# One batch of four of a mixed weight is built on VectorE instead of GpSimd

## The chip, the cores and the metric

The kernel is one program on 1 core of a Trainium2 chip. The metric is its device time in microseconds, the median of several runs. The engines are TensorE (PE in the profile, with its weight loads as PEld), VectorE (DVE), ScalarE (ACT), GpSimd (POOL) and SyncE (SP).

## The reference, cut to what matters

The whole computation is a transformer of four layers over x of 16 batches, 128 tokens and 128 features, with a conditioning vector of 8 numbers for each batch. Layer 0 reads, in short:

```python
x = x + _L0_attn_ref(_L0_cond_ref(x, cond_8, ...), Wq, Wk, Wv, Wo, ...)
x = x + _L0_ffn_ref(_L0_cond2_ref(x, cond_8, weight, mask, bias), w_gate, w_up, w_down)
```

The attention has 16 heads of 8 features. What the change touches belongs to the second line: `_L0_cond2_ref` multiplies the tokens of batch b by a weight that is a mixture of 8 matrices `weight[g]` (128x128) with the factors `cond_8[b, g]`, times a common `mask`. As the kernel writes it, transposed, with W8[g] = weight[g] * mask:

```python
WBOT[b] = sum(cond_8[b, g] * W8[g] for g in range(8))   # 16 batches, 128x128 each
y[b] = x[b] @ WBOT[b] + bias
```

## The kernel before

Activations lie in SBUF with the features on the partitions, 16 batches of 128 tokens in columns, worked on in NC = 4 chunks n of 4 batches (512 columns). The program is one list of steps, `order`, written while the kernel is built. Each engine walks the same list and issues its own part of each step in that order, so a step that stands earlier in the list stands earlier in every engine's queue. Waits between engines are semaphores, and buffers in rings (`Ring`, take and give) carry the signal after which they may be used again.

`in_order` makes the list as a software pipeline. An item is a list of stages. In each round one new item starts, and then every item that is under way does its next stage, the youngest first.

In the attention of layer 0 (`mh_attn(0, ...)`) an item is half of a group of heads: 4 chunks x 4 groups j x 2 halves = 32 items. The stages of one, with their lines:

- scores: TensorE, four products (L1660) into two PSUM banks of the ring RA, which has four banks. The keys are masked copies `kb`, made by GpSimd (L2721, four instructions for each two items, ring of three).
- row maximum and exponential: VectorE reduces both banks (L2251, twice) and subtracts the maximum in the first one (L2254); ScalarE takes exponentials of the second bank straight from PSUM (L1960, four), and of the first from SBUF (L1963). The banks come free after L2254 and after L1960.
- turn: TensorE transposes (L1587, L1588), ScalarE copies to SBUF (L1968).
- values and sums: TensorE (L1676, L1680).
- in every second item VectorE takes a reciprocal and multiplies (L2261, L2263), and at the end of a chunk TensorE projects (L1687) and VectorE adds the result to X (L2266).

Between the head items stand items for the next chunk: the conditioned weight (VectorE L2159, TensorE L1609, VectorE L2164, TensorE L1615), queries and keys (TensorE L1625, L1626, VectorE L2146), and values (VectorE L2217, TensorE L1631, VectorE L2244).

Beside the heads runs other work, one piece for each head item. `beside_heads` appends it to the first stage, behind the scores: first `wmask` (VectorE, L2269, which makes W8), then the 32 `wbot` steps (b = 0, 4, 8, 12, and for each b all g = 0 to 7), the last two in the 32nd item. In items 3 and on there is also a step of the feed-forward weights' quantization (`fq`, VectorE, L2275 to L2287), or of the routing (L2185 to L2210, and the multiply-add of L2146 on SM). So on VectorE whatever a head item has beside it stands before the row maximum of the item before.

A `wbot` step is GpSimd's alone. It multiplies W8[g], spread over four batches, by their four factors spread over 128 columns (L2731, a 128x512 product), for g > 0 into a scratch tile of the ring RWB, and then adds this to WBOT (L2735, also 128x512). WBOT is read by `cond2` (L1700), four products for each chunk, the first of which stand behind the last head items.

Of the kernel before, what the change touches and what calls it, by code (L numbers as in the profile page):

```python
# [115 lines left out]
def bc_mid(ap, n):  # L116
    return ap.rearrange("p (a b) -> p a b", a=1).broadcast_to([ap.shape[0], n, ap.shape[1]])
# [26 lines left out]
def build(nc, xT, cst, l0b, w8, b2, fw, fd, l1c, moe1, l1f, moe2, moe3, l2f, moe4, l3f, xs, ys, out):  # L144
    with ExitStack() as ctx:
# [29 lines left out]
        def c(name, rows=128):  # L175
            a, w = CL[name]
            return CC[0:rows, a:a + w]
# [31 lines left out]
        def tick(name, by=1):  # L209
            s = S_(name)  # L210
            counts[name] += by
            return s, counts[name]
# [5 lines left out]
        def step(kind, **at):  # L218
            order.append((kind, at))
            return at  # L220
# [353 lines left out]


        WBOT = A1[:, 8192:10240].rearrange("p (b o) -> p b o", b=16)
        RWB = Ring([A1[:, 10240 + 512 * k:10752 + 512 * k] for k in range(2)])
        WUG = BW[:, 6144:6912].rearrange("p (n o) -> p n o", o=128)
        WDN = BW[:, 6912:7296].rearrange("p (n o) -> p n o", o=128)

        def wbot_steps():
            def masked():
                sig["wmask"] = tick("wmask")
                step("wmask")
            steps = [masked]
            for b in range(0, NB, 4):
                for g in range(8):
                    def go(b=b, g=g):
                        at = step("wbot", b=b, g=g, mask=sig["wmask"], prev=sig.get(("wb", b)), tmp=RWB.take() if g else None)
                        at["part"] = sig["wb", b] = sig["wbot"] = tick("wbot_pool")  # L590
                        if g:
                            at["acc"] = sig["wb", b] = sig["wbot"] = tick("wbot_pool")
                            RWB.give(at["tmp"], at["acc"])
                    steps.append(go)
            return steps
# [35 lines left out]

        for n in range(NC):
            def c2(n=n):
                at = step("cond2", n=n, x=sig["x0", n], wbot=sig["wbot"], pa=RA.take(),
                          yfree=sig["Yfree", n])
                at["mm"] = sig["wbot_over"] = tick("c2_mm")
                at["y"] = sig["y0b", n] = tick("c2_y")
                RA.give(at["pa"], at["y"])
            items.append(([("x0", n)], [c2], ("y0b", n)))
# [937 lines left out]
        def _(e):  # L1577
# [27 lines left out]
            for kind, at in order:  # L1605
# [88 lines left out]
                elif kind == "cond2":  # L1694
                    over(at["pa"])
                    w.wait_ge(*at["wbot"])
                    w.wait_ge(*at["x"])
                    for j in range(4):
                        b = 4 * at["n"] + j
# [434 lines left out]
        def _(e):  # L2134
# [17 lines left out]
            for kind, at in order:  # L2152
# [114 lines left out]
                elif kind == "wmask":  # L2267
                    w.wait_ge(*loaded["w8"])
                    e.tensor_tensor(W8, W8, bc_mid(c("maskT"), 8), ALU.mult).then_inc(sig["wmask"][0], 1)  # L2269
                elif kind == "fq":  # L2270
                    k, mx, iv = at["k"], at["mx"], at["iv"]
                    r3 = at["raw"].rearrange("p (n k) -> p n k", k=32)
# [423 lines left out]
        def _(e):  # L2696
# [6 lines left out]
            for kind, at in order:  # L2703
# [18 lines left out]
                    i.then_inc(at["t"][0], 1)  # L2722
                elif kind == "wbot":
                    b, g = at["b"], at["g"]
                    to = WBOT[:, b:b + 4, :]
                    yb = COND.rearrange("p (b g) -> p b g", g=8)[:, b:b + 4, g]
                    part = v4(at["tmp"].ap) if g else to
                    w.wait_ge(*at["mask"])
                    if g:
                        over(at["tmp"])  # L2730
                    e.tensor_tensor(part, bc_mid(W8[:, g, :], 4), bc_last(yb, 128), ALU.mult).then_inc(at["part"][0], 1)  # L2731
                    if g:
                        w.wait_ge(*at["part"])
                        w.wait_ge(*at["prev"])
                        e.tensor_tensor(to, to, part, ALU.add).then_inc(at["acc"][0], 1)  # L2735
                elif kind == "f0_magic":
                    w.wait_ge(*loaded["cst2"])
# [144 lines left out]
```

## Time and profile before

| | us |
|---|---|
| median of 3 runs | 1372.43 |
| lowest and highest | 1371.03, 1373.96 |
| the profiled execution, its own time | 1373.96 |
| its span (first to last instruction) | 1372.10 |
| granted clock over the span | 0.978 of full |
| PE busy | 1245.3 |
| DVE busy | 839.9 |
| ACT busy | 666.9 |
| POOL busy | 283.7 |

How to read it: busy time is a sum over the whole span, of stages with different limits. Times in views of the trace count from the start of the span. An idle time in brackets at the end of a timeline row is that of the engine just before the row, with the instruction that ended it. Matmuls are pipelined, so rows of TensorE can overlap.

### The profile page before, as it was taken

What the parts mean: (1) busy time and instruction counts of PE and PEld (TensorE: products, weight loads), DVE (VectorE), ACT (ScalarE), POOL (GpSimd) and SP (SyncE); (2) the same over time, 40 slices, a digit from 0 to 9 for tenths busy, and PEclk for the clock granted to TensorE, in tenths of its full rate; (3) what the DMA queues carried; (4) which work ended last, traced back from release to release, by engine and by line L of the source; (5) the groups of instructions that cost most, each with busy time, mean ns of one, the idle gap of its engine ahead of it and who ended that gap; (6) DMA issues with size and microseconds to landing.
All of it is one profiled execution on the core that took longest, in us unless ns stands there. A gap on an engine that the chain in (4) does not pass through costs nothing.

```text
span 1372.1 us, 26279 instructions
## 1 busy us (share of the span) xinstructions
PE 1245.3 (91%) x9327; PEld 965.1 (70%) x9327; DVE 839.9 (61%) x1781; ACT 666.9 (49%) x1346; POOL 283.7 (21%) x379
## 2 busy tenths in 40 slices
PE   6999962889999899999999999899999999998999
PEld 2555621468788799887878887698889655556777
DVE  4888678564555567567776564666554666754242
ACT  2666687345434234443444444244444466655553
POOL 5877300210004143220000022233400211100000
PEclk9999986999999999999999999999999999999999
DMA  9000100501222122105034002032020000000000
GB/s 320 2 2 1 43 36 0 207 1 62 104 105 89 57 84 77 43 18 208 1 133 180 1 16 60 25 110 64 28 87 1 1 2 1 2 1 1 0 16 16
DMA packets 42892, 75.69 MB, mean 55 GB/s; under 512 B 3848, under 2 KB 33808, under 8 KB 41872
## 3 DMA queue, kind: packets, MB, share of 16 engines
q1 hardware_dynamic: 38672, 65.62, 13.2%
q0 software_dynamic: 4096, 8.40, 2.1%
q8 instruction: 80, 1.31, 0.4%
q14 instruction: 44, 0.36, 0.1%
HBM read 59.72 MB, written 14.29 MB: 54 GB/s over the span
## 4 chain that ended last, share of the span: by engine, by line
PE 75%; DVE 13%; ACT 7%; issue 3%; DMA 1%; DVEq 1%; POOL 0%; ACTq 0%; SPq 0%; POOLq 0%
PE bank L1811 8%; PE bank L1822 7%; PE bank L1807 7%; PE bank L1866 5%; PE bank L1660 4%; PE bank L1798 4%; PE bank L1587 4%; PE bank L1876 3%; PE bank L1592 3%; PE bank L1593 3%; PE bank L1594 2%; PE bank L1791 2%; PE bank L1793 2%; PE bank L1792 2%; PE bank L1676 2%
## 5 line engine op out<-in xcount | busy, mean ns | idle before, releaser
L2059 ACT ACTIVATE SC<-bank 128x512 f32<-128x512 f32 x192 | 114.4, 596 | 222.4 <-PE bank L1807 124.8
L2146 DVE SCALAR_TENSOR_TENSOR SC<-bank,SM,SC 128x512 f32<-128x512 f32 x128 | 95.8, 748 | 122.6 <-PE bank L1811 101.0
L1822 PE MATMUL bank<-A,SC 128*128 x1024 | 137.0, 277 | 7.8 <-DVE SC L2146 7.1
L1807 PEld LDWEIGHTS bank<-X,SC 128*128 128x128 f32 x1024 | 127.0, 193 | 19.3 <-issue 13.0
L1811 PE MATMUL bank<-X,SC 128*128 128x128 f32 x1024 | 137.3, 277 | 3.3 <-DVE SC L2420 2.7
L1807 PE MATMUL bank<-X,SC 128*128 128x128 f32 x1024 | 136.9, 277 | 3.2 <-ACT SC L2043 2.5
L1822 PEld LDWEIGHTS bank<-A,SC 128*128 128x128 f32 x1024 | 125.5, 192 | 17.1 <-issue 16.3
L1811 PEld LDWEIGHTS bank<-X,SC 128*128 128x128 f32 x1024 | 125.4, 193 | 5.4 <-DVE SC L2420 5.2
L1866 PE MATMUL bank<-A 128*128 128x128 f32 x736 | 100.2, 280 | 11.2 <-DVE A L2570 6.2
L1960 ACT ACTIVATE A<-bank,SM 128x128 f32<-128x128 f32 x256 | 73.8, 383 | 58.0 <-DVE SM L2251 57.8
L1866 PEld LDWEIGHTS bank<-A 128*128 128x128 f32 x736 | 90.1, 193 | 15.4 <-ACT A L2084 8.9
L2721 POOL TENSOR_SCALAR A<-A,CC 128x256 f32<-128x256 f32 (+1 forms) x128 | 55.0, 450 | 214.0 <-DVE A L2238 108.8
L2043 ACT ACTIVATE SC<-A 128x512 f32 x128 | 80.6, 630 | 28.5 <-PE bank L1811 22.8
L2771 POOL DMA_INDIRECT A<-ys,POSI x64 | 62.7, 980 | 130.0 <-PE bank L1860 38.4
L2759 POOL DMA_INDIRECT xs<-CC,POSI x64 | 64.2, 1003 | 115.8 <-DVE POSI L2549 28.1
L2251 DVE TENSOR_REDUCE SM<-bank 128x4 f32<-128x512 f32 x128 | 81.8, 680 | 7.9 <-PE bank L1660 6.4
L2400 DVE TENSOR_TENSOR SC<-bank,SC 128x512 f32<-128x512 f32 x64 | 44.3, 692 | 62.5 <-PE bank L1793 52.1
L1660 PE MATMUL bank<-A 64*128 64x512 f32 (+1 forms) x256 | 73.7, 653 | 8.3 <-POOL A L2721 3.7
L1587 PEld LDWEIGHTS bank<-CC,A 128*128 128x128 f32 x408 | 46.8, 142 | 43.9 <-issue 16.1
L1876 PE MATMUL bank<-BW,A 128*128 x552 | 77.2, 277 | 0.0
L1592 PE MATMUL bank<-R 128*128 128x512 f32 x176 | 69.4, 394 | 7.6 <-DVE SC L2146 6.1
L2746 POOL TENSOR_TENSOR SM<-SM 128x32 f32<-128x32 f32 x32 | 8.3, 259 | 314.4 <-DVE SM L2146 312.5
(322 smaller groups left out, 2586.1 us busy)
## 6 DMA issues: line engine op xcount, KB each, us to landing
A<-in_moe SPq DMA_DIRECT2D x36, 768.0 KB, 10.3
A<-xs SPq DMA_DIRECT2D x20, 256.0 KB, 4.0
ys<-A SPq DMA_DIRECT2D x20, 256.0 KB, 2.3
BW<-in_l1f SPq DMA_DIRECT2D x2, 2048.0 KB, 7.5
BW<-in_l2f SPq DMA_DIRECT2D x1, 3456.0 KB, 12.2
BW<-in_l1c SPq DMA_DIRECT2D x1, 3072.0 KB, 17.3
BW<-in_l3f SPq DMA_DIRECT2D x1, 2816.0 KB, 9.7
A<-in_l1c SPq DMA_DIRECT2D x1, 2560.0 KB, 8.7
```

Source lines behind the costliest of these rows:

```text
L1587: e.transpose(o[:, cut(r)], i[:, cut(r)], ident)
L1592: e.matmul(o, wh, hi, start=start, stop=False)
L1660: m = e.matmul(pa.ap, q[rows, a:a + 128], kb[rows, b:b + 512], start=at["i"] == 0, stop=True)
L1807: m = e.matmul(at["pg"].ap[:, cut(q)], wx[:, cut(q)], x, start=True, stop=True)
L1811: m = e.matmul(at["pu"].ap[:, cut(q)], wx[:, cut(4 + q)], x, start=True, stop=True)
L1822: m = e.matmul(o, at["h"].ap[:, cut(q)], W[:, bass.ds(r + (1024 + 128 * q), 128)], start=k == 0 and q == 0, stop=k == 1 and q == 3)
L1866: m = e.matmul(at["pa"].ap[:, cut(q)], at["wt"].ap[:, cut(q)], at["x"].ap, start=True, stop=True)
L1876: m = e.matmul(o, at["ht"].ap[:, cut(q)], BW[:, bass.ds(r + (dn + 128 * q), 128)], start=q == 0, stop=q == nk - 1)
L2043: e.activation(at["wx"].ap[0][:, 0:512], MOE_AT[at["L"]][:, bass.ds(r, 512)], ACT.Identity).then_inc(at["g"][0], 1)
L2059: e.activation(at["h"].ap, at["pg"].ap, ACT.Gelu_apprx_tanh).then_inc(at["gelu"][0], 1)
L2146: return e.scalar_tensor_tensor(out=o, in0=a, scalar=s, in1=b, op0=o1, op1=o2)
L2251: e.tensor_reduce(m[:, 4 * x:4 * x + 4], v4(pa.ap), AX, ALU.max, negate=True).then_inc(at["max"][x][0], 1)
```

## The change

In each `wbot` step, GpSimd does batches b+1 to b+3 (128x384 instead of 128x512) and VectorE does batch b itself: one 128x128 instruction, a `tensor_scalar` for g = 0 and a `scalar_tensor_tensor` (W8[g] times the factor, plus WBOT) for g > 0. Both have two semaphore counters now, `wbot_dve` for VectorE and `wbot_pool` for GpSimd, each engine waits for its own earlier sum alone, and `cond2` waits for both. The scratch tiles have 384 columns instead of 512. `stt(o, a, s, b, o1, o2)` is `e.scalar_tensor_tensor`, as VectorE's other code uses it.

```diff
--- before.py
+++ after.py
@@ -574,7 +574,7 @@
 
 
         WBOT = A1[:, 8192:10240].rearrange("p (b o) -> p b o", b=16)
-        RWB = Ring([A1[:, 10240 + 512 * k:10752 + 512 * k] for k in range(2)])
+        RWB = Ring([A1[:, 10240 + 384 * k:10624 + 384 * k] for k in range(2)])
         WUG = BW[:, 6144:6912].rearrange("p (n o) -> p n o", o=128)
         WDN = BW[:, 6912:7296].rearrange("p (n o) -> p n o", o=128)
 
@@ -586,10 +586,12 @@
             for b in range(0, NB, 4):
                 for g in range(8):
                     def go(b=b, g=g):
-                        at = step("wbot", b=b, g=g, mask=sig["wmask"], prev=sig.get(("wb", b)), tmp=RWB.take() if g else None)
-                        at["part"] = sig["wb", b] = sig["wbot"] = tick("wbot_pool")
+                        at = step("wbot", b=b, g=g, mask=sig["wmask"], prev=sig.get(("wb", b)), prev_pool=sig.get(("wb3", b)),
+                                  tmp=RWB.take() if g else None)
+                        at["t"] = sig["wb", b] = sig["wbot"] = tick("wbot_dve")
+                        at["part"] = sig["wb3", b] = sig["wbot_pool"] = tick("wbot_pool")
                         if g:
-                            at["acc"] = sig["wb", b] = sig["wbot"] = tick("wbot_pool")
+                            at["acc"] = sig["wb3", b] = sig["wbot_pool"] = tick("wbot_pool")
                             RWB.give(at["tmp"], at["acc"])
                     steps.append(go)
             return steps
@@ -631,7 +633,7 @@
 
         for n in range(NC):
             def c2(n=n):
-                at = step("cond2", n=n, x=sig["x0", n], wbot=sig["wbot"], pa=RA.take(),
+                at = step("cond2", n=n, x=sig["x0", n], wbot=sig["wbot"], wbot_pool=sig["wbot_pool"], pa=RA.take(),
                           yfree=sig["Yfree", n])
                 at["mm"] = sig["wbot_over"] = tick("c2_mm")
                 at["y"] = sig["y0b", n] = tick("c2_y")
@@ -1694,6 +1696,7 @@
                 elif kind == "cond2":
                     over(at["pa"])
                     w.wait_ge(*at["wbot"])
+                    w.wait_ge(*at["wbot_pool"])
                     w.wait_ge(*at["x"])
                     for j in range(4):
                         b = 4 * at["n"] + j
@@ -2267,6 +2270,15 @@
                 elif kind == "wmask":
                     w.wait_ge(*loaded["w8"])
                     e.tensor_tensor(W8, W8, bc_mid(c("maskT"), 8), ALU.mult).then_inc(sig["wmask"][0], 1)
+                elif kind == "wbot":
+                    b, g = at["b"], at["g"]
+                    y = COND[:, 8 * b + g:8 * b + g + 1]
+                    w.wait_ge(*at["mask"])
+                    if g == 0:
+                        e.tensor_scalar(WBOT[:, b, :], W8[:, g, :], y, None, ALU.mult).then_inc(at["t"][0], 1)
+                    else:
+                        w.wait_ge(*at["prev"])
+                        stt(WBOT[:, b, :], W8[:, g, :], y, WBOT[:, b, :], ALU.mult, ALU.add).then_inc(at["t"][0], 1)
                 elif kind == "fq":
                     k, mx, iv = at["k"], at["mx"], at["iv"]
                     r3 = at["raw"].rearrange("p (n k) -> p n k", k=32)
@@ -2722,16 +2734,16 @@
                     i.then_inc(at["t"][0], 1)
                 elif kind == "wbot":
                     b, g = at["b"], at["g"]
-                    to = WBOT[:, b:b + 4, :]
-                    yb = COND.rearrange("p (b g) -> p b g", g=8)[:, b:b + 4, g]
-                    part = v4(at["tmp"].ap) if g else to
+                    to = WBOT[:, b + 1:b + 4, :]
+                    yb = COND.rearrange("p (b g) -> p b g", g=8)[:, b + 1:b + 4, g]
+                    part = at["tmp"].ap.rearrange("p (b o) -> p b o", b=3) if g else to
                     w.wait_ge(*at["mask"])
                     if g:
                         over(at["tmp"])
-                    e.tensor_tensor(part, bc_mid(W8[:, g, :], 4), bc_last(yb, 128), ALU.mult).then_inc(at["part"][0], 1)
+                    e.tensor_tensor(part, bc_mid(W8[:, g, :], 3), bc_last(yb, 128), ALU.mult).then_inc(at["part"][0], 1)
                     if g:
                         w.wait_ge(*at["part"])
-                        w.wait_ge(*at["prev"])
+                        w.wait_ge(*at["prev_pool"])
                         e.tensor_tensor(to, to, part, ALU.add).then_inc(at["acc"][0], 1)
                 elif kind == "f0_magic":
                     w.wait_ge(*loaded["cst2"])
```

## Rows read from the trace of the kernel before

**Rows 1.** The page, part 1: busy time and share of the span of each engine.

```profile
PE 1245.3 (91%) x9327; PEld 965.1 (70%) x9327; DVE 839.9 (61%) x1781; ACT 666.9 (49%) x1346; POOL 283.7 (21%) x379
```

**Rows 2.** The chain that ended last between 26 and 147 us, shares by line.

```profile
by line: PE bank L1660 24.9%; PE bank L1587 17.5%; PE bank L1676 10.4%; PE bank L1680 8.0%; PE bank L1625 5.3%; PE bank L1588 4.9%; ACT A L1960 4.6%; PE bank L1626 4.3%; DVE SM L2251 3.0%; PE bank L1609 2.5%; PE bank L1715 2.4%; PE bank L16
```

**Rows 3.** Windows: us, busy (count) of PE, PEld, DVE, ACT, POOL, clock, DMA.

```profile
26.00:147.00 121.00, 114.58 (x1291) 68.82 (x1289) 101.00 (x222) 79.02 (x207) 96.21 (x117) 0.99 0.07 19
...
118.00:142.00 24.00, 22.87 (x308) 14.04 (x300) 21.75 (x84) 18.91 (x52) 23.37 (x29) 1.00 0.01 3
```

**Rows 4.** Groups of GpSimd by line and shape, 26 to 160 us: count, busy, mean.

```profile
L2735 POOL TENSOR_TENSOR A<-A 128x512 f32<-128x512 f32 x28 | 36.6, 1307 | 2.2
L2731 POOL TENSOR_TENSOR A<-A,CC 128x512 f32<-128x512 f32 x32 | 34.8, 1087 | 0.0
L2721 POOL TENSOR_SCALAR A<-A,CC 128x256 f32<-128x256 f32 x57 | 27.1, 495 | 22.6 <-PE bank L1588 9.0 <-DVE A L2146 8.2 <-PE bank L1660 5.3
```

**Rows 5.** Timeline of GpSimd: start, us, line, operation, idle before.

```profile
61.89 1.27 POOL L2735 TENSOR_TENSOR A<-A 128x512 f32<-128x512 f32 x1
63.13 1.76 POOL L2731 TENSOR_TENSOR A<-A,CC 128x512 f32<-128x512 f32 x1
...
133.92 1.85 POOL L2721 TENSOR_SCALAR A<-A,CC 128x256 f32<-128x256 f32 x4
...
146.28 1.28 POOL L2735 TENSOR_TENSOR A<-A 128x512 f32<-128x512 f32 x1
```

**Rows 6.** Timeline of TensorE.

```profile
54.22 1.13 PE L1660 MATMUL bank<-A 64*128 64x512 f32 x4 [1.62 <-ACT A L1960]
...
56.62 1.13 PE L1660 MATMUL bank<-A 64*128 64x512 f32 x4 [0.24 <-issue]
...
73.17 1.10 PE L1625 MATMUL bank<-Y,CC 128*128 128x512 f32 x2 [0.91 <-ACT A L1960]
...
88.94 1.13 PE L1660 MATMUL bank<-A 64*128 64x512 f32 x4 [0.18 <-ACT A L1960]
...
138.41 1.13 PE L1660 MATMUL bank<-A 64*128 64x512 f32 x4
...
146.60 1.13 PE L1660 MATMUL bank<-A 64*128 64x512 f32 x4
...
152.79 1.16 PE L1700 MATMUL bank<-X,A 128*128 128x128 f32 x8
```

**Rows 7.** Timeline of ScalarE (ACT).

```profile
55.37 1.14 ACT L1960 ACTIVATE A<-bank,SM 128x128 f32<-128x128 f32 x4 [0.78 <-DVE SM L2251]
...
87.65 1.14 ACT L1960 ACTIVATE A<-bank,SM 128x128 f32<-128x128 f32 x4
...
137.04 1.14 ACT L1960 ACTIVATE A<-bank,SM 128x128 f32<-128x128 f32 x4 [0.54 <-DVE SM L2251]
```

**Rows 8.** Timeline of VectorE (DVE).

```profile
49.94 0.29 DVE L2263 TENSOR_TENSOR A<-bank,A 128x128 f32<-128x128 f32 x1
50.15 1.54 DVE L2281 TENSOR_TENSOR A<-A,SM 128x768 f32<-128x768 f32 x1
...
61.99 1.99 DVE L2287 TENSOR_TENSOR A<-A,SM 128x768 f32<-128x768 f32 x1
...
69.96 0.69 DVE L2266 TENSOR_TENSOR X<-bank,X 128x512 f32<-128x512 f32 x1 [2.40 <-PE bank L1687]
...
96.05 1.25 DVE L2281 TENSOR_TENSOR A<-A,SM 128x384 f32<-128x384 f32 x1
...
113.37 0.55 DVE L2287 TENSOR_TENSOR A<-A,SM 128x384 f32<-128x384 f32 x1
...
118.70 0.96 DVE L2261 RECIPROCAL A<-bank 128x128 f32<-128x128 f32 x1 [0.60 <-PE bank L1680]
...
121.69 0.57 DVE L2185 CAST IDB<-CC 128x128 bf16<-128x128 f32 x1
...
135.39 0.42 DVE L2146 SCALAR_TENSOR_TENSOR SM<-SM 128x32 f32<-128x32 f32 x1
```

## The prediction

> **What bounds the kernel now.** I read the page first. TensorE is busy for 91% of the span and GpSimd (POOL) for 21% [rows 1]: over the whole kernel TensorE is the bound, and GpSimd is not. But the change touches one stage, the attention of layer 0 with its 32 head steps, from about 26 to 147 us. So the windows of that stage come next. There VectorE (DVE) is busy 101.00 of 121 us, GpSimd 96.21, TensorE 114.58, and between 118 and 142 us VectorE is busy 21.75 and GpSimd 23.37 of 24 us, with TensorE at full granted clock, 1.00 (2.4 GHz) [rows 3]. Both engines between which work is moved are nearly full. Which one matters is told by the chain that ended last: in this stretch its shares are TensorE's, then ACT's exponential L1960 at 4.6% and VectorE's row maximum L2251 at 3.0%, and no GpSimd line is among the shares shown [rows 2].
>
> Is GpSimd on the path anywhere? It makes two things that TensorE needs: the masked keys (L2721), and WBOT. The last four-instruction group of masked keys starts at 133.92, ends 1.85 us later at 135.77, and feeds a scores product that starts at 146.60, after the one at 138.41 has used the group before it. WBOT is finished at 146.28 + 1.28 = 147.56 [rows 5] and first read by L1700 at 152.79 [rows 6]. GpSimd has 5.2 us to spare at WBOT and about 11 us at the keys. What is taken from it shortens nothing directly.
>
> VectorE has no such room. TensorE idles where a scores product waits for a PSUM bank, which comes free when ACT has done the four L1960, which wait for VectorE's L2251 of the same head. At 54.22 TensorE had idled 1.62 us for L1960. At 56.62 it starts 0.11 us after the L1960 that began at 55.37 (55.37 + 1.14 = 56.51), and that one had waited 0.78 us for VectorE. At 88.94 it is the same (87.65 + 1.14 = 88.79), and so at one earlier product, near 44 us. At 138.41 the product starts 0.23 us after the end of the L1960 that began at 137.04, itself held up 0.54 us by VectorE [rows 6, 7]. The handoff takes 0.10 to 0.15 us in the cases where TensorE idles, so about 0.1 us is slack.
>
> **The change, part by part.** GpSimd's two instructions per step go from four batches to three, from 128x512 to 128x384. Before they took 34.8 us (x32, mean 1.087) and 36.6 us (x28, mean 1.307) [rows 4]. I scale by elements, an estimate: 0.79 and 0.95 us at the undisturbed 1.05 and 1.27. That frees some 17 us of GpSimd, worth nothing by itself, since its cover is the 5.2 and 11 us above. The added wait of L1700 for a second semaphore is also worth nothing: VectorE's last slice, at the 32nd head step, stands in its queue before row maxima that finish before 152.79. The two scratch buffers only shrink.
>
> VectorE gets 32 instructions of 128x128, one in each head step: 4 multiplications by a scalar and 28 multiply-adds (scalar_tensor_tensor) of WBOT. Each is queued before the row maximum of the head before, on the chain above. Its own occupancy: L2263, 128x128 on VectorE, has 0.29 us and the next instruction starts 0.21 us after it (49.94 to 50.15) [rows 8]. I take 0.21.
>
> To that comes a wait. The new instructions read two operands from SBUF, and so does L2281 (a tile of A times a strip of SM). At 96.05 a 128x384 L2281 took 1.25 us, while L2287 on the same shape with GpSimd idle took 0.55 at 113.37: 0.70 more. At 61.99 the 128x768 L2287 took 1.99 us. Its undisturbed time, from 0.55 plus 384 elements at (0.55-0.29)/256 us each, is 0.94: 1.05 more. In that moment GpSimd ran L2735 from 61.89 to 63.16, and then an L2731 that took 1.76 instead of 1.05 [rows 5, 8]. VectorE stood until GpSimd's instruction ended, ran, and held up GpSimd's next one. At 50.15 it is 1.54 - 0.94 = 0.60 more, for the 128x128 cast at 121.69 0.57 - 0.29 = 0.28. For the 128x32 multiply-add at 135.39, 0.42 against 0.19 (0.29 less 96 elements) is 0.23 more. Mean of the five: 0.57 us. That a multiply-add of two SBUF operands does it too is told by the last of these.
>
> The Trainium skill, SBUF — State Buffer, section "Who interferes with whom", says the same of the pair of ports that VectorE and GpSimd share: an instruction of VectorE with two SBUF inputs and one of GpSimd that reads SBUF exclude each other for the whole instruction. By that rule the move cannot be free while GpSimd works; by the rows alone it is 0.23 to 1.05 us for each that meets it. The Trainium skill, Perfetto Trace Analysis, section "Optimizing Scalar/DVE Operations", adds that offloading between these two might not help for this reason; the trace agrees in these five rows.
>
> How often do they meet? If the new instruction comes at a random moment, its mean wait is the sum over GpSimd's instructions of count times duration squared, over twice the 121 us: (32 x 0.79^2 + 28 x 0.95^2 + 57 x 0.46^2) / 242 = (20.0 + 25.3 + 12.1) / 242 = 0.24 us (0.46 is one of the four instructions of the 1.85 us at 133.92). Bounds: no wait, 0; always a meeting like those measured, 0.57. I take 0.24, since most of those measured were long enough to be caught and GpSimd's instructions are now shorter. One new instruction then costs w = 0.21 + 0.24 = 0.45 us, between 0.21 and 0.78. All 32 are 14.4 us of VectorE.
>
> How many lie on the path? I count them at each place where TensorE waits for VectorE, from the last idle moment of VectorE before it: before the product near 44 us, one; before 54.22, one; before 56.62, one more; at 69.96 VectorE adds to X after an idle time of 2.40 us, and the step's new instruction stands between it and the row maximum whose L1960 lets TensorE start at 73.17 after 0.91 us of idling [rows 6, 8]: one; before 88.94 one, and one more for the product after it; the same addition to X one chunk later: one. Then from 118.70 on VectorE has no idle time in its queue until that release at 138.41 is past. The new instructions of head steps 22 to 27 stand there before the row maximum that releases 138.41: six. Together 1+1+1+1+2+1+6 = 13. The other 19 fall into idle times of VectorE, or where TensorE has 0.4 to 2 us in hand. 13 x 0.45 = 5.85 us.
>
> Off goes slack: 0.1 at 138.41 and about 0.4 at the others together, 0.5 (an estimate). Off goes relief: the waits of VectorE's old instructions on this path (0.60 at 50.15, 0.28 at 121.69, 0.23 at 135.39: 1.1) shrink with GpSimd's instructions to about three quarters: 0.3. Sum: 5.85 - 0.5 - 0.3 = +5.05 us. A check from capacity: 118 to 142 us has 2.25 us of VectorE free and gets 8 x 0.45 = 3.6, so it must grow by at least 1.35 us; the path count gives 6 x 0.45 - 0.1 = 2.6. Behind the stage everything moves as a block, for I see nothing with its own due time.
>
> The profiled execution was 1373.96 us (span 1372.1), 1.5 above the median of 1372.43. The sum makes it 1379.0; against the median, 1372.43 + 5.05 = 1377.5.
>
> **The rivals.** (A) The forecast: 1377.5, own range 1375.2 to 1379.5.
>
> (B) VectorE absorbs it. For: 19 of 32 are already counted as hidden, and GpSimd gets gaps in which nobody waits for it. Then w is 0.21 at the same 13 places: 2.7 - 0.8 = +1.9, 1374.4; if places drop out as well, 1372.4. Against: GpSimd is busy 23.37 of 24 us in the densest stretch now [rows 3], and its work there falls only by a fifth or so.
>
> (C) The waits bunch. VectorE's new instruction is caught each time, as the long ones were (w = 0.78): 13 x 0.78 = 10.1, less 0.5 is +9.6, 1382.0. For: five rows of such waits. Against: the means of rows 4 (1.087 and 1.307 against 1.05 and 1.27) show that most of GpSimd's instructions met nobody, and the new ones are short.
>
> (D) Faster: the relief outweighs the load. Mechanism: GpSimd catches up with its queue and idles while VectorE runs its long two-operand instructions, so all 1.1 us of old waits on the path go, and L2281 at 96.05 and L2287 at 61.99 lose another 1.75 between them: up to -2.85, 1369.6. It decides only if w at the 13 places is nearly nothing, under 2.85/13 = 0.22, that is without any wait and with some of the places hidden. For it: both engines share what they contend for. Against: the occupancy of 0.21 alone eats it. The other way to be faster, that GpSimd was late, is excluded by 5.2 and 11 us of room.
>
> (E) The Trainium skill, GPSIMD Engine Reference, section "Engine selection", prefers VectorE for elementwise work, GpSimd being about twice as slow with two inputs. That is an advantage in engine time: some 17 us of GpSimd freed against 32 x 0.21 = 6.7 us of VectorE. As a time it would show only through (D), and is counted there.
>
> **How the numbers follow.** No change can be told from a change under 0.2%, 2.7 us here. Chances: A 0.45, B 0.32, C 0.15, D 0.08. A and C end slower; of B 0.05 too, when w lies between; of D 0.05 is faster and 0.03 within. Slower 0.65, same 0.30, faster 0.05. The likeliest is A: 1377.5. The range leaves out the upper part of C and most of D, and B below 1373: 1373.0 to 1381.5.
>
> **What would show it.** Right: 32 new DVE rows of 128x128, many longer than 0.3 us, their ends on ends of GpSimd's instructions; GpSimd's two groups at about 0.8 and 0.95 us; the first L1700 about 5 us later than 152.79, and the time behind it unchanged; VectorE's idle time between 118 and 145 us gone, and TensorE's waits for L1960 longer there. Wrong: the new rows all near 0.2 us (B); TensorE's waits for L1960 not longer, so that the count of 13 was too high; the first L1700 earlier (D); or a second place that moves, behind 170 us, which the block shift excludes.

## The result, and the profile after

The changed kernel took 1379.76 us (median of the first 6 runs, 1378.61 to 1387.59), the kernel before 1372.16 in the same series. The ratio of its runs to those of the kernel before on the same chip is 1.007, 95% interval 1.0052 to 1.0089: 9.6 us slower, between 7.1 and 12.2. It was run again beside the experiments: over all 25 runs, the first six among them, its median is 1381.83 and its range 1376.71 to 1387.59. So the direction was forecast and the size was not: +5.05 us against 7.6 (medians) to 9.6 (ratio). The median of the first six lies in the range of 1373.0 to 1381.5, the ratio times 1372.43, 1382.0, lies outside.

The spread itself is new: 11 us over 25 runs, where the 73 runs of the kernel before beside them have 6 (1368.71 to 1374.57). It goes with TensorE's granted clock. The runs with a granted clock of 0.980 over the span took 1376.7 to 1379.7 us, those with 0.975 or 0.974 took 1384.5 to 1387.6. The kernel before lies at 0.978 or above in 72 of the 73. A part of this lies far behind the stage of the change: the profiled execution of the kernel before was granted 0.91 of full clock from 260 to 280 us and 0.93 from 455 to 480 and from 615 to 640, that of the changed kernel 1.00 in all three. So one execution compared with one other can be off by some us, and where it matters below the stage is compared by itself.

The page after, part 1, as in [rows 1]:

```profile
PE 1245.9 (90%) x9327; PEld 963.3 (70%) x9327; DVE 852.2 (62%) x1813; ACT 667.2 (48%) x1346; POOL 268.1 (19%) x379
```

The windows after, as in [rows 3], and one more stretch:

```profile
118.00:142.00 24.00, 21.93 (x286) 13.98 (x284) 23.58 (x88) 16.42 (x44) 23.26 (x34) 1.00 0.01 2
142.00:160.00 18.00, 14.19 (x156) 8.76 (x154) 12.88 (x26) 9.92 (x27) 3.09 (x4) 0.81 0.01 2
```

The same stretch of the kernel before:

```profile
142.00:160.00 18.00, 17.12 (x233) 12.10 (x234) 11.42 (x19) 13.41 (x35) 5.40 (x5) 1.00 0.01 2
```

From 118 to 142 us VectorE has gone from 21.75 to 23.58 us busy. From 142 to 160 TensorE was granted 0.81 of full clock, where it had 1.00. GpSimd's groups by shape, 24 to 170 us, as in [rows 4]:

```profile
L2747 POOL TENSOR_TENSOR A<-A 128x384 f32<-128x384 f32 x28 | 29.2, 1042 | 2.2
L2743 POOL TENSOR_TENSOR A<-A,CC 128x384 f32<-128x384 f32 x32 | 26.8, 839 | 0.0
```

VectorE's new instructions, the 28 multiply-adds and the 4 multiplications:

```profile
L2149 DVE SCALAR_TENSOR_TENSOR A<-A,CC 128x128 f32<-128x128 f32 x28 | 14.7, 526 | 0.0
...
L2278 DVE TENSOR_SCALAR A<-A,CC 128x128 f32<-128x128 f32 x4 | 1.7, 428 | 0.0
```

GpSimd's two groups are at 0.839 and 1.042 us (0.79 and 0.95 forecast). The new instructions have means of 0.526 and 0.428 us.

TensorE's timeline, as in [rows 6]. The product of 54.22 is now at 54.83, 56.62 at 58.11, 88.94 at 91.36, 118.56 at 121.00, 138.41 at 145.01, and the first product of WBOT of 152.79 (L1703 now) at 162.24:

```profile
54.83 1.45 PE L1662 MATMUL bank<-A 64*128 64x512 f32 x4 [2.05 <-ACT A L1963]
...
58.11 1.51 PE L1662 MATMUL bank<-A 64*128 64x512 f32 x4
...
77.81 1.13 PE L1662 MATMUL bank<-A 64*128 64x512 f32 x4
...
91.36 1.13 PE L1662 MATMUL bank<-A 64*128 64x512 f32 x4 [0.73 <-ACT A L1963]
...
121.00 1.13 PE L1662 MATMUL bank<-A 64*128 64x512 f32 x4
...
145.01 2.08 PE L1662 MATMUL bank<-A 64*128 64x512 f32 x4 [2.94 <-DVE A L2257]
...
151.39 1.12 PE L1689 MATMUL bank<-A,CC 128*128 128x512 f32 x2
...
162.24 1.16 PE L1703 MATMUL bank<-X,A 128*128 128x128 f32 x8
```

At 145.01 TensorE had idled 2.94 us, and its scores step (the row of four) then took 2.08 us instead of 1.13. The granted clock was 0.56 of full from 144 to 146 us and 0.50, which is the lower level of 1.2 GHz, from 146 to 150. From there to the projection L1689 at 151.39 it needs 6.38 us. Before, the same work took from 138.41 to 141.94, 3.53 us:

```profile
118.56 1.13 PE L1660 MATMUL bank<-A 64*128 64x512 f32 x4
...
141.94 1.13 PE L1687 MATMUL bank<-A,CC 128*128 128x512 f32 x2
```

So the delay grows in three parts: 2.44 us up to 118.56, 4.16 more up to 138.41 (6.60 in all), and 2.85 more at the lower clock (9.45 in all at the first product of WBOT).

What VectorE did in the idle time, and GpSimd beside it:

```profile
136.75 1.28 DVE L2254 TENSOR_REDUCE SM<-bank 128x4 f32<-128x512 f32 x2
...
138.55 1.17 DVE L2149 SCALAR_TENSOR_TENSOR A<-A,CC 128x128 f32<-128x128 f32 x1
138.56 1.00 POOL L2747 TENSOR_TENSOR A<-A 128x384 f32<-128x384 f32 x1
...
139.52 0.89 POOL L2743 TENSOR_TENSOR A<-A,CC 128x384 f32<-128x384 f32 x1
...
139.64 0.80 DVE L2207 TENSOR_SCALAR SM<-SM 128x16 f32<-128x16 f32 x1
...
140.47 0.25 DVE L2209 RECIPROCAL SM<-SM 128x16 f32<-128x16 f32 x1
140.48 1.00 POOL L2747 TENSOR_TENSOR A<-A 128x384 f32<-128x384 f32 x1
...
140.76 0.76 DVE L2211 TENSOR_TENSOR SM<-SM 128x16 f32<-128x16 f32 x1
...
141.44 0.83 POOL L2743 TENSOR_TENSOR A<-A,CC 128x384 f32<-128x384 f32 x1
141.55 0.76 DVE L2213 TENSOR_SCALAR SM<-SM 128x32 f32<-128x32 f32 x1
142.34 0.19 DVE L2149 SCALAR_TENSOR_TENSOR SM<-SM 128x32 f32<-128x32 f32 x1
142.35 1.04 POOL L2747 TENSOR_TENSOR A<-A 128x384 f32<-128x384 f32 x1
142.45 1.28 DVE L2254 TENSOR_REDUCE SM<-bank 128x4 f32<-128x512 f32 x2
...
143.77 1.14 ACT L1963 ACTIVATE A<-bank,SM 128x128 f32<-128x128 f32 x4 [3.07 <-DVE SM L2254]
```

The row maxima (L2254) start at 136.75 and next at 142.45. Between them stand the new instruction (1.17 us) and five tiny instructions that make the routing weights from 16 or 32 columns. Each depends on the one before. The new instruction ends when GpSimd's L2747 (138.56 to 139.56) has ended, L2207 ends at 140.44, just before GpSimd's next begins, L2211 at 141.52 and L2213 at 142.31, each time at the end of an instruction of GpSimd or in the gap before the next. So three of the five wait for what is left of an instruction of GpSimd. The reciprocal L2209 and the last one, L2149, do not. In the kernel before, this chain happened to run beside the masked keys, 0.46 us each [rows 5, the row at 133.92], and ended with the row at 135.39 [rows 8]:

```profile
134.35 0.16 DVE L2204 TENSOR_SCALAR SM<-SM 128x16 f32<-128x16 f32 x1
134.55 0.25 DVE L2206 RECIPROCAL SM<-SM 128x16 f32<-128x16 f32 x1
134.84 0.20 DVE L2208 TENSOR_TENSOR SM<-SM 128x16 f32<-128x16 f32 x1
135.07 0.28 DVE L2210 TENSOR_SCALAR SM<-SM 128x32 f32<-128x32 f32 x1
```

1.46 us from 134.35 to 135.81 there, 2.89 us from 139.64 to 142.53 here: 1.43 us more.

### The profile page after: what moved, and what is told of

Its sections match the earlier page's. It is cut to its first block, busy times and chain, and to the rows that moved or that the text cites. A ratio compares the mean times of both kernels' runs of the same rounds, so it can differ in the third digit from the quotient of the medians.

```text
span 1378.9 us, 26311 instructions
## 1 busy us (share of the span) xinstructions
PE 1245.9 (90%) x9327; PEld 963.3 (70%) x9327; DVE 852.2 (62%) x1813; ACT 667.2 (48%) x1346; POOL 268.1 (19%) x379
## 4 chain that ended last, share of the span: by engine, by line
PE 71%; DVE 16%; ACT 7%; issue 4%; DVEq 1%; DMA 1%; POOL 0%; ACTq 0%; SPq 0%; POOLq 0%
PE bank L1814 7%; PE bank L1825 7%; PE bank L1810 7%; PE bank L1869 5%; PE bank L1801 4%; PE bank L1662 4%; PE bank L1589 3%; PE bank L1879 3%; PE bank L1594 3%; PE bank L1596 2%; PE bank L1595 2%; PE bank L1794 2%; DVE SM L2254 2%; PE bank L1796 2%; PE bank L1795 2%
## 5 line engine op out<-in xcount | busy, mean ns | idle before, releaser
L2149 DVE SCALAR_TENSOR_TENSOR SC<-bank,SM,SC 128x512 f32<-128x512 f32 x128 | 95.9, 749 | 122.1 <-PE bank L1814 95.6
L2254 DVE TENSOR_REDUCE SM<-bank 128x4 f32<-128x512 f32 x128 | 81.9, 681 | 8.5 <-PE bank L1662 7.2
L1879 PEld LDWEIGHTS bank<-BW,A 128*128 128x128 f32 x552 | 69.3, 192 | 2.0 <-issue 1.9
## 6 DMA issues: line engine op xcount, KB each, us to landing
BW<-in_l2f SPq DMA_DIRECT2D x1, 3456.0 KB, 12.2
```

Source lines behind the costliest of these rows:

```text
L1879: m = e.matmul(o, at["ht"].ap[:, cut(q)], BW[:, bass.ds(r + (dn + 128 * q), 128)], start=q == 0, stop=q == nk - 1)
L2149: return e.scalar_tensor_tensor(out=o, in0=a, scalar=s, in1=b, op0=o1, op1=o2)
L2254: e.tensor_reduce(m[:, 4 * x:4 * x + 4], v4(pa.ap), AX, ALU.max, negate=True).then_inc(at["max"][x][0], 1)
```

## The experiments

All ratios are against runs of the kernel before on the same chip, in the same series. "Head stage" below is the time from the third scores step (33.23 us before) to the first product of WBOT (152.79), in the profiled execution: 119.6 us before, 129.1 after the change. It leaves out what differs in start and rest from one execution to the next, but it is read from one execution of each kernel.

**r1: GpSimd's share left out.** Batches b+1 to b+3 are zeros, VectorE's instructions stay.

```diff
+ e.memset(WBOT[batches b+1 to b+3], 0.0).then_inc(t_wzero[0], 1)     # once, at the start
- GpSimd: both instructions of every wbot step
```

> The changed kernel, but GpSimd's share of WBOT (batches b+1 to b+3) is left out: zeros are written there once at the start, so that share of the computation is missing. VectorE's 32 instructions stay. Port theory (the loss comes from waits of VectorE for GpSimd's running instruction, which end in idle TensorE and then in half clock): the 28 multiply-adds fall from a mean of 0.53 us to 0.34 (the value of those that met nobody), the old waits go as well, no TensorE idling over 2 us in the head stage, time 1370 to 1374 us. Occupancy theory (the 32 instructions' own time on the path is what costs): about 11 places x 0.26 = +2.9 at least stays and, with the clock drops unchanged, the time is 1376 to 1380 us.

Measured: 1375.2 us (12 runs), ratio 1.0021 (1.0011 to 1.0031): +2.9 us. Head stage 120.6 us. VectorE's group of new instructions:

```profile
L2148 DVE SCALAR_TENSOR_TENSOR A<-A,CC 128x128 f32<-128x128 f32 x28 | 10.4, 372 | 0.0
```

The same 28 instructions take 0.372 us each, not 0.526. With GpSimd's share gone nearly nothing is left to wait for, so +2.9 us (1.5 to 4.2) is about what their occupancy costs. In the profiled execution only 1.1 us of it lies in the head stage; where the rest lies was not found. The port theory's time was 1.2 us too low, since it took no occupancy into account, and the occupancy theory's 1376 to 1380 was 0.8 too high.

**r2: the new instructions cannot wait.** VectorE reads one operand only.

```diff
- stt(WBOT[:, b, :], W8[:, g, :], y, WBOT[:, b, :], ALU.mult, ALU.add)
+ e.tensor_reduce(RED[:, k:k + 1], W8[:, g, :], AX, ALU.max)
```

> The changed kernel with each of VectorE's 32 new instructions replaced by a maximum over one 128x128 slice of W8, written to a column of its own: one SBUF operand, about the same length. Batch b of each four is left out of WBOT (zeros written once at the start). GpSimd's share is as in the changed kernel. Port theory: the new instructions show about 0.25 us each with no spread, VectorE's old two-operand instructions still wait, time 1373 to 1376 us. Occupancy theory: as the changed kernel, 1379 to 1382 us.

Measured: 1378.99 us (5 runs), ratio 1.0051 (1.0038 to 1.0064): +7.0 us. The port theory as I had put it falls here, and the time is at the lower end of the occupancy theory's. The new instructions take 0.274 us and meet nobody, and yet most of the loss is there. The trace suggested another cause. VectorE's routing chain:

```profile
137.47 0.73 DVE L2210 TENSOR_SCALAR SM<-SM 128x16 f32<-128x16 f32 x1
138.24 0.25 DVE L2212 RECIPROCAL SM<-SM 128x16 f32<-128x16 f32 x1
138.53 0.76 DVE L2214 TENSOR_TENSOR SM<-SM 128x16 f32<-128x16 f32 x1
139.31 0.76 DVE L2216 TENSOR_SCALAR SM<-SM 128x32 f32<-128x32 f32 x1
140.11 0.19 DVE L2152 SCALAR_TENSOR_TENSOR SM<-SM 128x32 f32<-128x32 f32 x1
```

and TensorE afterwards:

```profile
142.78 1.13 PE L1665 MATMUL bank<-A 64*128 64x512 f32 x4 [1.71 <-DVE A L2260]
```

The chain has moved from 134.35 to 137.47 and takes 2.83 us instead of 1.46: here it is old instructions that wait, because the new ones push them onto GpSimd's instructions of 0.83 to 1.0 us. This gave the theory that r10 and r14 test. It does not explain all of this run: the head stage is 122.7 us, 3.1 more than before, and the other 4 us of the +7.0 lie outside it. TensorE also kept full clock after its 1.71 us of idling.

**r3: GpSimd's share alone.** VectorE's 32 instructions are gone, batch b is zero.

> The changed kernel without VectorE's 32 instructions: batch b of each four is left out of WBOT (zeros written once at the start), GpSimd does three batches of 384 columns as in the changed kernel. Both theories: GpSimd's shorter instructions alone cost nothing, 1370.5 to 1372.5 us, a little faster than before as the old waits shrink (0.3 us). Rival (the shift in phase between the two engines is itself the cause of the convoy of small routing instructions near 140 us): 1375 us or more.

Measured: 1371.8 us (11 runs), ratio 0.9997 (0.9988 to 1.0006). Head stage 119.5 us. Shortening GpSimd's instructions is worth nothing clear of the noise, as forecast (between 1.6 us faster and 0.8 slower).

**r4: VectorE's instructions on top of the kernel before.**

```diff
+ VectorE, wbot: stt(DUP[:, b // 4, :], W8[:, g, :], y, DUP[:, b // 4, :], ALU.mult, ALU.add)   # own scratch
  GpSimd, wbot: four batches, 128x512, as before
```

> The kernel before, GpSimd's four batches untouched, plus VectorE's 32 instructions of the changed kernel, which write to a scratch tile of their own (their result is not used; the load of l1b waits for them too). Port theory: GpSimd's instructions are long again (1.05 and 1.27 us), so the multiply-adds wait longer, mean about 0.6 us, and the time is 1381 to 1386 us. Occupancy theory: the same 32 instructions cost the same as in the changed kernel, 1379 to 1382 us.

Measured: 1383.22 us (5 runs), ratio 1.0075 (1.0062 to 1.0088): +10.3 us. The multiply-adds have a mean of 0.609 us. The port theory's span was met. Relieving GpSimd gave back little: head stage 129.9 us against 129.1, and +10.3 against +9.6 us is no difference clear of noise.

**r6: what the kernel before itself loses.** GpSimd's work on WBOT is left out there.

> The kernel before with GpSimd's WBOT work left out (zeros written once at the start, so that part of the computation is missing). Shows what VectorE's old two-operand instructions lose to GpSimd in the kernel before. Port theory: 1370 to 1371.5 us, 0.5 to 2 us faster than before; next to r1_no_gpsimd (1375.2) it gives the pure price of the 32 instructions' occupancy. Occupancy theory says nothing else here: 1372 us, no difference.

Measured: 1372.07 us (12 runs) against 1372.69, ratio 0.9996 (0.9988 to 1.0005). The interval is from 1.6 us faster to 0.7 slower, and the head stage is 119.0 us, 0.5 less than before. So the old waits of VectorE (1.1 us counted in the prediction) cost about 0.5 us in the stage and at most 1.6 in time. The 2.85 that rival D hoped for was not to be had.

**r7: the new instruction behind the row maximum.**

```diff
- attn[k] = (it[0], [lambda: (f0(), extras)] + it[1][1:], it[2])
+ attn[k] = (it[0], [lambda: (f0(), extras), lambda: (f1(), wbot_v)] + it[1][2:], it[2])
```

> The changed kernel with VectorE's new instruction queued behind the row maximum of its own head step instead of ahead of that of the step before (the last one stays as it was). The same instructions, the same load on both engines. Port theory: a wait now delays the row maximum only where VectorE's queue is full anyway (118 to 142 us), so one third to a half of the loss goes: 1375 to 1379 us. Occupancy theory: full queue, the order in it does not matter, 1379 to 1382 us.

Measured: 1378.25 us (6 runs), ratio 1.0042 (1.0026 to 1.0057): +5.8 us, within the 1375 to 1379 of the port theory. Head stage 126.7 us, and TensorE still idles 2.02 us ahead of the same scores product.

**r8 and r12: VectorE's other side work of the kernel before in another place.** r8 queues it behind the row maximum, r12 two head steps later:

```diff
- beside_heads[3 + k].append(f)
+ beside_heads[5 + k].append(f)        # r12
```

> The kernel before (no work moved), with VectorE's other side work of the head steps (the quantization of the feed-forward weights and the routing) queued behind the row maximum of its own head step instead of ahead of that of the step before. If that side work with its waits for GpSimd lies on the path as the chain shows at 50.15 us (1.54 us for L2281, then the row maximum), the time falls by 0.5 to 3 us to 1369.5 to 1371.5 us. Rival: the queue is full, the order in it does not matter, 1372 us.

> The kernel before (no work moved), with all of VectorE's other side work two head steps later (from step 5 instead of 3). It takes L2281 from in front of the row maximum that ends the wait of TensorE at 54.22 us (1.62 us) and the routing weights from in front of the one for 138.41. Path theory: 0.5 to 1.5 us faster, 1371 to 1371.8 us. Rival: the same pieces meet other row maxima as late, no change or slower, as r8_before_small_behind was (+2).

Measured: r8 1374.57 us, ratio 1.0015 (1.0007 to 1.0024): +2.1 us, slower where the path theory had it faster. r12 1378.58 us (5 runs), ratio 1.0043 (1.0029 to 1.0057): +5.9 us, though not one instruction was added to the kernel before. In r12 the chain stands at 144.40:

```profile
144.40 1.21 DVE L2204 TENSOR_SCALAR SM<-SM 128x16 f32<-128x16 f32 x1
145.64 0.25 DVE L2206 RECIPROCAL SM<-SM 128x16 f32<-128x16 f32 x1
145.93 0.69 DVE L2208 TENSOR_TENSOR SM<-SM 128x16 f32<-128x16 f32 x1
146.65 0.18 DVE L2210 TENSOR_SCALAR SM<-SM 128x32 f32<-128x32 f32 x1
146.87 1.14 DVE L2146 SCALAR_TENSOR_TENSOR SM<-SM 128x32 f32<-128x32 f32 x1
```

and TensorE behind it:

```profile
150.48 1.65 PE L1660 MATMUL bank<-A 64*128 64x512 f32 x4 [3.13 <-DVE A L2254]
```

It takes 3.61 us from 144.40 to 148.01, since GpSimd is at its 128x512 instructions, and TensorE idles 3.13 us and then has the lower clock for a part of the scores step (1.65 us instead of 1.13). The head stage is 125.3 us, 5.7 more than before, and only 0.9 of that stands ahead of the chain (the scores step of 143.95 is at 144.62, in an execution whose third step is at 32.99). So a loss of this kind can be had without the change. r12 moved all of the side work, not this chain alone. Here the path theory was wrong by more than 6 us.

**r10: the chain moved away in the changed kernel.**

```diff
- beside_heads[3 + k].append(f)
+ beside_heads[30 if f is rt[4] else 3 + k].append(f)
```

> The changed kernel with one piece of side work moved: the five small instructions that make the routing weights (L2207 to L2213 and the multiply-add on SM, 4.0 us from 138.55 with VectorE's new instruction, before the row maximum at 142.45) are issued beside head step 30 instead of 27. Convoy theory (each of these two-port instructions waits for a whole instruction of GpSimd, and because the new instruction ahead of them shifts them onto GpSimd's, the wait of 2.94 us and the half clock behind it follow): the time falls by 3 to 6 us to 1374 to 1378 us. Queue theory (VectorE is simply full from 118 to 142 us): 2.5 us at most, 1378 to 1380 us.

Measured: 1376.15 us (7 runs), ratio 1.0029 (1.0017 to 1.0041): +4.0 us where the change as it is has +9.6. Head stage 124.2 us instead of 129.1. The chain runs after GpSimd's last instruction on WBOT:

```profile
151.60 0.17 DVE L2207 TENSOR_SCALAR SM<-SM 128x16 f32<-128x16 f32 x1
...
152.09 0.17 DVE L2211 TENSOR_TENSOR SM<-SM 128x16 f32<-128x16 f32 x1
152.30 0.18 DVE L2213 TENSOR_SCALAR SM<-SM 128x32 f32<-128x32 f32 x1
```

Its instructions take 0.17 to 0.19 us, the reciprocal 0.25. There is no long wait before the scores product, now at 142.8. The move does two things at once: the chain no longer waits, and its own 1.1 to 1.5 us are gone from the queue ahead of that product. The kernel before with the chain moved in the same way was not run; its TensorE did not idle ahead of 138.41 [rows 6], so little is to be expected there.

**r14: both, the new instructions cannot wait and the chain is moved.**

> r2_one_operand (VectorE's 32 instructions replaced by a maximum over one 128x128 slice, batch b of each four left out) with the routing weights' five instructions moved to head step 30. r2 was 1379.0, 7.0 us above before, though its new instructions take 0.27 us and never wait. Chain theory (the 7 are mostly the routing chain, which waited three times 0.75 us in front of a row maximum, and the 1.7 us idle time of TensorE behind it): 1373 to 1375.5 us. Occupancy theory: 1377 to 1379 us.

Measured: 1376.09 us (9 runs), ratio 1.0021 (1.0011 to 1.0031): +2.9 us, against +7.0 with the chain in place (r2). That is the same +2.9 as in r1, in which hardly anything could wait either. The median is 0.6 us above the chain theory's span, and the kernel before had 1373.02 in that series. But the head stage is 122.1 us against 122.7 in r2. In the two profiled executions the move takes only 0.6 us off the stage, and most of the 4.1 us between the two medians lies elsewhere. So the pair r2 and r14 does not carry the chain theory; the changed kernel and r10 do (129.1 and 124.2).

**r11: the split for the first 16 steps only.**

```diff
+ b1 = b + 1 if b < 8 else b        # GpSimd does all four batches from b = 8 on, VectorE none
```

> The changed kernel for the first 16 of the 32 steps (b = 0 and 4), the kernel before for the last 16 (b = 8 and 12: GpSimd does all four batches). The traces put +2.4 us of the loss before 118 us and +7 between 118 and 151. So 1373.5 to 1375.5 us by the port theory; by occupancy alone (half of the instructions, half of r1's +3) 1373.5 as well; if the loss were spread evenly over the steps, 1376 to 1377.

Measured: 1376.11 us (8 runs), ratio 1.0028 (1.0017 to 1.0038): +3.8 us, 0.6 above the expected span, and in that of the losses spread evenly (1376 to 1377). That is more than the +2.4 us by which the changed kernel's trace is late when the first half of the stage is over (91.36 against 88.94). Head stage 122.1 us, 2.6 more than before.

**r5, r9 and r13: keeping TensorE's clock.** Products of the identity were put ahead of the two scores products that wait long (at 54.83 and 145.01). r5 had 5 and 8, r9 (shown) and r13 2 and 3; r13 took a bank of another ring.

```diff
  def s_scores(...):
+     if (n, j, half) in ((3, 2, 0), (0, 3, 1)):
+         keep_on(3 if n else 2)
```

> The changed kernel plus idle products of TensorE (identity times identity into a spare bank, 0.22 us each at full clock) in front of the two scores products that follow the long waits: 5 before the one that came at 54.83 us, 8 before the one at 145.01. Nothing else is changed. If the half clock after those waits is a part of the loss of its own (it cost about 2.9 us behind 145 and 0.9 behind 55 in the changed kernel's trace), the time falls by 2 to 4 us to 1375.5 to 1378 us, the spread over runs shrinks from 9 us to about 3, and the granted clock stays 1.00 from 142 to 160 us. If the clock only hides under waits that VectorE sets anyway, it stays at 1379 to 1382 us.

> As r5_keep_clock, whose products took 0.91 us each instead of the 0.22 supposed and were far too many (4.56 us for five), but now 2 before the scores product at 54.83 us and 3 before the one at 145.01: 1.8 and 2.7 us of work in waits of 2.05 and 2.94 us. Clock theory (half clock behind the two waits costs about 3.7 us of its own): 1375.5 to 1378 us and less spread than the 11 us of the changed kernel. Rival (the half clock is covered by VectorE's queue, which is as late anyway): 1379 to 1382 us.

> As r9_keep_clock_sized (2 idle products before the scores product that came at 54.83 us, 3 before the one at 145.01, 0.91 us each), but into a bank of the ring that the value products use and that is free at that moment, so that TensorE does them inside the waits. Clock theory: granted clock 1.00 from 142 to 160 us, no scores product over 1.2 us, time 2 to 4 us below the changed kernel's: 1375.5 to 1378.5, spread over runs under 5 us. Rival (the time behind the wait is set by VectorE, not by TensorE's clock): 1379 to 1382 us.

Measured: r5 1394.28 us (1.0151, 1.0131 to 1.0171), r9 1386.61 us (1.0099, 1.0083 to 1.0114), r13 1387.61 us (1.0111, 1.0095 to 1.0126): slower all three, and no theory had this. In r5 I had the length of a product wrong (0.91 us, not 0.22). In r9 and r13 the bank was not free: what frees it, ScalarE's copy (L1973) in r9 and VectorE's multiplication (L2270) in r13, is as late as everything behind VectorE. The products near 145 came after the wait, not in it:

```profile
53.41 1.98 PE L1722 MATMUL bank<-CC 128*128 128x512 f32 x4
55.55 1.13 PE L1666 MATMUL bank<-A 64*128 64x512 f32 x4 [0.16 <-ACT A L1967]
...
58.55 1.13 PE L1666 MATMUL bank<-A 64*128 64x512 f32 x4 [0.85 <-DVE A L2261]
...
145.01 4.54 PE L1722 MATMUL bank<-CC 128*128 128x512 f32 x6 [2.65 <-DVE A L2270]
149.48 1.13 PE L1666 MATMUL bank<-A 64*128 64x512 f32 x4
...
153.01 1.12 PE L1693 MATMUL bank<-A,CC 128*128 128x512 f32 x2
```

The head stages are 136.8, 131.1 and 130.0 us, so of r13's loss against the changed kernel only 0.9 us lies there. Its profiled execution, 1381.68, is the fastest of its four (the others 1387.2 to 1388.6), and where the rest lies was not found.

Three readings remain of use. Near 55 us the two products did lie inside the wait and the clock stayed full: the scores product comes at 58.55, 24.7 us behind the third scores step (33.8 in this execution). In the changed kernel it comes at 58.11, 25.0 behind its 33.1. The half clock is worth 0.3 us there; VectorE sets the time. Near 149, at full clock, the work to the projection takes 3.53 us (149.48 to 153.01) against 6.38 at half clock in the changed kernel: 2.85 us. And these 2.85 us do come off at the first product of WBOT. Counted from the third scores step, the scores product is later than in the changed kernel by 10.5 us in r5, 4.8 in r9 and 3.8 in r13, the first product of WBOT by 7.7, 2.0 and 0.9. That they come off the whole time too was not shown.

## Why the prediction was wrong in size

**Right.** GpSimd is not on the path, and its relief is worth nothing clear of the noise (r3). The sign and its cause, VectorE's queue ahead of the row maxima, hold: VectorE's instructions without GpSimd's share cost 2.9 us (r1), GpSimd's without VectorE's nothing (r3). GpSimd's new durations were 0.839 and 1.042 us against 0.79 and 0.95. The mean wait of a new multiply-add was 0.19 us (0.526 less the 0.34 of those that met nobody, as at 145.44) against 0.24. Behind the stage things move as a block as far as can be told. In the two profiled executions the first product of WBOT is 9.45 us later and the end of the span 6.8, but the one before was 1.5 us above its median and the one after 1.1 below.

**The occupancy** was 0.26 us (43.80 to 44.06 in the changed kernel's VectorE timeline), not 0.21. Its price is 2.9 us by the times of r1 and r14. By the count it should have been 13 x 0.26 = 3.4 less 0.5 of slack, 2.9 (2.4 with the 11 places that are left of the 13, see below), so it is right for its size.

**The count of 13** was wrong in two places. After the addition to X the next instruction in VectorE's queue is the row maximum; the new instruction comes behind it, since items of the next chunk stand in between. The products near 77 and 110 us have the same delay as those before them (75.93 to 77.81 is +1.88; 61.75 to 63.62 had +1.87 already). By that trace those two places cost nothing.

**The waits of the new instructions** were put at 13 x 0.24 = 3.1 us. The difference of r10 (4.0) and r14 (2.9) gives 1.1, good to some 2 us, so it is also compatible with 3.1; their head stages differ by 2.1.

**The step that failed** is a pair of terms. The first is "Off goes relief: the waits of VectorE's old instructions on this path (...) shrink with GpSimd's instructions to about three quarters: 0.3". Such a wait is not a property of an instruction but of the moment. Two of the three rows in that term did not shrink by a quarter but lost their wait whole: the one of 50.15 took 0.95 us (at 51.36) instead of 1.54, the cast of 121.69 took 0.22 instead of 0.57. The third was the last of the chain of five routing instructions. The chain had waited little because it ran beside the masked keys. In the changed kernel it comes later by what the new instructions add, meets instructions of 0.83 and 1.0 us, and three of its five wait: 2.89 us instead of 1.46, with the new instruction's own 1.17 ahead of it. So the term is +1.43 less 0.94, +0.5 us and not -0.3. The second was put at nothing: that TensorE, after the longer wait, comes back at half clock. It costs 2.85 us.

In the prediction's own parts: up to 118 us it had 7 x 0.45 - 0.4 = 2.75, and the trace shows 2.44. From there to the product of 138.41 it had 2.6, and the trace shows 4.16, of which 1.43 are the chain's waits and 2.73 the rest. The clock, at nothing in the forecast, adds 2.85. That makes 9.45 us in the stage, beside 9.6 by the times. Moving the chain takes 5.6 us off the time of the changed kernel (9.6 to 4.0, good to some 3 us) and 4.9 off its head stage. An estimate from the parts gives as much: 2.85 for the clock, 1.43 for the waits and some 1.5 for the chain's own time, 5.8.

**Of the rivals,** C (the waits bunch) had the right total, 1382.0, by luck, and not the mechanism: its 0.78 for each new instruction was 0.45 in the mean (0.26 and 0.19), and the bunch is in the old ones. D's relief is there in the rows (the two long ones of 61.99 and 96.05 took 0.95 and 0.55 us in the changed kernel, at 63.66 and 98.95, all of the 1.75 it counted), and the time rose even so; r3 and r6 show how little there was to gain. That the clock could fall behind a longer wait stood in no term.

**Open.** Whether all of the 2.85 us at the lower clock reach the whole time: they do reach the first product of WBOT (r5, r9, r13), but no run kept the clock at that place without other work in front. Where r2's and r13's time outside the head stage comes from. And the chain moved in the kernel before, which would part its waits from its own time.

The Trainium skill, SBUF — State Buffer, section "Who interferes with whom", says that issue order, not the shape of an instruction, decides who is blocked. The trace agrees: the same 128x16 instruction took 0.16 us or 1.21 us (L2204 in the kernel before at 134.35 and in r12 at 144.40, where it came 0.09 us behind the start of a GpSimd instruction and ended with it, at 145.61 against 145.57).

## What to carry to other kernels

Where an instruction of one engine waits for the running one of another, as VectorE's did here for GpSimd's, the price of a small instruction is what is left of the other engine's instruction that it meets. A chain of dependent small instructions can pay it again and again, here at three links of five. Keep such chains off stretches in which GpSimd runs long instructions, and out of the queue ahead of what TensorE waits for. When work is put into a queue that is full, ask not only what the new instructions cost, but what the old ones behind them will meet at their new time. And ask whether the engine that waits at the end keeps its clock through the longer wait. Moving work from an engine that had room to one that had none cost time here, though the second needs less of its own for it: 0.26 us a slice without waits, where GpSimd's busy time fell by 15.6/32 = 0.49 us a slice.

## What the runs showed of the hardware that was not expected

- The five routing instructions on 16 or 32 columns took 1.46 us beside GpSimd's 0.46 us instructions, 1.10 us without GpSimd (136.81 to 137.91 in r1), 2.89 beside its 128x384 instructions and 3.61 beside its 128x512 ones.
- A `tensor_reduce` over 128x128 with one SBUF operand took 0.274 us in the mean over 32 beside a busy GpSimd: it never waited.
- One product of identity by 128x512 in float32 took 0.91 us at full clock (r5: five in 4.56 us). It shows as two instructions in the trace, so the rows of four of a scores step are two products, not the four named above, with 0.57 us each.
- After 2.94 us of idling, behind a stretch at full clock, TensorE ran at half clock from 145.01 to about 151 us. After 2.05 us (54.83) it also fell, between 55 and 56 us, while the product of 54.83 ran (1.45 us). After 1.62 us in the kernel before and 1.71 us in r2 it did not.
